# Light attention on one core: a step's three projections in one run, the output product in one run, and the next batch's rows turned behind the transposes

## The reference

```python
def local_attn(x, Wqkv, Wout):            # H = 8 heads of 64, windows of W = 64 rows
    q, k, v = jnp.split(x @ Wqkv.T, 3, axis=-1)
    q, k, v = map(towin, (q, k, v))
    ke, ve = (expand(k), expand(v))       # own window and its two neighbours
    sim = jnp.einsum('bhnid,bhnjd->bhnij', q, ke) * SCALE
    sim = jnp.where(valid, sim, -1e9)
    attn = jax.nn.softmax(sim, axis=-1)
    o = jnp.einsum('bhnij,bhnjd->bhnid', attn, ve)
    return o @ Wout.T
light = local_attn(_ln(x, ln_w, ln_b), Wqkv, Wout_l)
out = ... + light                          # and a "heavy" part on routed rows
```

## Time and profile before

| | |
|---|---|
| median of 3 runs | 1851.25 us (1850.41 to 1852.17) |
| span of the profiled execution | 1853.5 us; no other time of that execution is given |
| mean granted clock of TensorE | 0.970 |
| busy: PE, PEld, DVE, ACT, POOL | 90%, 69%, 78%, 78%, 41% of the span |
| light stage f1, first to last copy of `late` | 503.9 to 999.1 us |
| light stage f2, first to last copy of `late` | 1245.8 to 1732.2 us |

### The profile page before, as it was taken

How to read it: one execution, slowest core, us unless ns; L and a number is a source line. 1 busy time by engine, 2 the same in 40 slices (tenths; PEclk the granted TensorE clock), 3 DMA queues, 4 the chain that set the end, 5 groups by cost and what they waited for, 6 DMA issues and landing times. The chain is left out here.

```text
span 1853.5 us, 67967 instructions
## 1 busy us (share of the span) xinstructions
PE 1676.8 (90%) x27513; PEld 1287.6 (69%) x27513; DVE 1449.6 (78%) x3461; ACT 1437.3 (78%) x4100; POOL 753.0 (41%) x842
## 2 busy tenths in 40 slices
PE   3888898886899999999997996879999999999797
PEld 1444444443688888888886774658888888888686
DVE  8999999998677678877887766747777777789674
ACT  4989999996788888888774666658888888877464
POOL 2010000000255444455446866425454545455694
PEclk7999999998999999999999997989999999999999
DMA  6565556551001010101012000000101010001211
GB/s 194 140 155 146 149 124 148 132 149 28 13 15 25 14 26 14 26 14 26 14 26 48 2 2 1 1 12 15 25 14 26 15 25 18 22 14 25 48 47 47
DMA packets 80040, 91.95 MB, mean 50 GB/s; under 512 B 11696, under 2 KB 67984, under 8 KB 79728
## 3 DMA queue, kind: packets, MB, share of 16 engines
q1 hardware_dynamic: 78432, 87.15, 19.0%
q10 hardware_dynamic: 1296, 0.44, 0.1%
HBM read 39.68 MB, written 31.10 MB: 38 GB/s over the span
## 5 line engine op out<-in xcount | busy, mean ns | idle before, releaser
L1519 POOL TENSOR_TENSOR f1l_pn<-f1l_p,f1l_rs 128x512 f32<-128x512 f32 (+1 forms) x256 | 207.9, 834 | 259.3 <-DVE f1l_rs L1206 258.2
L1519 POOL TENSOR_TENSOR f2l_pn<-f2l_p,f2l_rs 128x512 f32<-128x512 f32 (+1 forms) x256 | 207.9, 834 | 248.8 <-DVE f2l_rs L1206 248.7
L1078 ACT ACTIVATE f2l_p<-f2l_sm,f2l_nb 128x192 f32<-128x192 f32 x512 | 214.7, 444 | 43.9 <-DVE f2l_nb L1199 43.9
L1078 ACT ACTIVATE f1l_p<-f1l_sm,f1l_nb 128x192 f32<-128x192 f32 x512 | 214.8, 444 | 42.0 <-DVE f1l_nb L1199 42.0
L417 PE MATMUL r_acc<-r_pr,r_vp 128*32 128x128 f32 (+2 forms) x3584 | 197.9, 338 | 6.9 <-DVE r_pr L630 6.0
L527 ACT ACTIVATE r_pr<-r_far 128x1536 f32<-128x1536 f32 x128 | 195.4, 1526 | 3.3 <-PE r_far L401 3.0
L622 DVE SCALAR_TENSOR_TENSOR r_pr<-r_pr,k_lo,r_cap 128x512 f32<-128x512 f32 x256 | 180.7, 746 | 11.0 <-ACT r_pr L527 10.9
L630 DVE TENSOR_SCALAR r_pr<-r_pr,k_hi,k_lo 128x768 f32<-128x768 f32 x256 | 164.5, 684 | 0.0
L527 ACT ACTIVATE r_pr<-r_near 128x1024 f32<-128x1024 f32 x128 | 139.6, 1091 | 1.1 <-PE r_near L388 1.1
L1524 POOL MEMSET k_rtz<- 128x132 f32 x1 | 0.2, 208 | 337.3 <-POOLq L688 337.3
L417 PEld LDWEIGHTS r_acc<-r_pr,r_vp 128*32 128x32 f32 x3584 | 89.1, 112 | 49.7 <-issue 31.2
(11 more groups left out here) (505 smaller groups left out, 5158.7 us busy)
## 6 DMA issues: line engine op xcount, KB each, us to landing
rbf_rows<-r_part SPq DMA_DIRECT2D x112, 128.0 KB, 2.3
r_qs<-rbf_rows SPq DMA_DIRECT2D x60, 192.0 KB
r_ks<-rbf_rows SPq DMA_DIRECT2D x60, 192.0 KB
f1l_vs<-f1l_vv SPq DMA_DIRECT2D x64, 128.0 KB, 2.4
f2l_vs<-f2l_vv SPq DMA_DIRECT2D x64, 128.0 KB, 2.4
rbf_rows<-r_part SPq DMA_DIRECT2D x16, 384.0 KB, 3.1
rbf_rows<-r_part SPq DMA_DIRECT2D x16, 256.0 KB, 3.2
out<-k_x SPq DMA_DIRECT2D x8, 512.0 KB, 3.2
```

What stands on the lines that cost most here:

```text
L1078: ins = nc.scalar.activation(p[:, u % 2, k, :], sm[:, u % 2, k // 2, k % 2 * PW:(k % 2 + 1) * PW], ACT.Exp, bias=nb[:, u % 2, k:k + 1], ac ...
L1519: ins = nc.gpsimd.tensor_tensor(pn[:, u % 2, at:at + HU * w].rearrange("p (k c) -> p k c", k=HU), p[:, u % 2, :, cols], r.broadcast_to([P, ...
```

## The change

On TensorE the three projections of a step now come first and one after another, into three banks: `pj`, `tp` and `xa[:, 1]`. The transposes of unit a then wait until `tp` has been emptied again by ScalarE, and the values of unit a wait for `xa[:, 1]`. The four chunks of the output product are one run into the first columns of `pj`. The transposes of unit b follow, and with i = 2 `turn_x`, now into `pj`. On ScalarE the first two copies out of the projections stand together ahead of the second exponential, the third one exponential later. On VectorE the residual stands behind the copies of unit a in every step.

```diff
         def bank(b, k):
             if b == 0 and (k <= 2 * HP or not C):
                 return (pj[:], tp[:], xa[:, 0, :], xa[:, 1, :])[k % 4]
-            return tp[:] if k == 0 else pj[:]
+            if b == 0 or k == 0:
+                return tp[:] if b == 1 else pj[:]
+            return (xa[:, 1, :], pj[:], tp[:])[k % 3]
+
+        def out_bank(t):
+            return pj[:, 0:P] if t < T - 1 else xa[:, 1, 0:P]
...
             def use(b, k):
                 at, par = bank(b, k), b % 2
+                t = NT * (b - 1) + (k - 1) // 3
                 if b == 0 and (k <= 2 * HP or not C):
                     wait(pe, s_pe, k - 4)
+                elif b == 0:
+                    pe.wait_ge(s_pe, k - 1)
+                elif k % 3 == 1:
+                    if t == 0:
+                        pe.wait_ge(s_pe, USES)
+                    wait(pe, s_la, t - 1)
+                    if t % NT == TURN_AT + 1 and b + 1 < B:
+                        pe.wait_ge(s_xe, b + 2)
+                elif k % 3 == 2:
+                    if t == 0:
+                        pe.wait_ge(s_xe, 2)
+                    wait(pe, s_pt, 2 * t)
                 else:
-                    pe.wait_ge(s_pe, USES * b + k - 1)
+                    if t == 0 and C:
+                        pe.wait_ge(s_re, 1)
+                    wait(pe, s_ov, 2 * t)
...
             def turn(n):
...
                 pe.wait_ge(s_nm, n + 1)
                 wait(pe, s_pt, n)
+                if u % 2 == 0 and b + 1 < B:
+                    pe.wait_ge(s_pe, USES * (b + 1) + 3 * (u // 2) + 2)
...
             def values(n):
...
-                if u % 2 == 0:
-                    wait(pe, s_la, NT * b + i)
+                if u % 2 == 0 and b + 1 < B:
+                    pe.wait_ge(s_pe, USES * (b + 1) + 3 * i + 3)
...
             def step(t):
                 b, i = t // NT, t % NT
                 more = b + 1 < B
-                ahead = i == TURN_AT and b + 2 < B
                 if more:
-                    use(b + 1, 3 * i + 1)
+                    for k in range(1, 4):
+                        use(b + 1, 3 * i + k)
                 turn(2 * t)
-                output(t - 1, (0,) if ahead else (0, 1))
-                if more:
-                    use(b + 1, 3 * i + 2)
-                if not ahead:
-                    output(t - 1, (2, 3))
+                output(t - 1)
                 turn(2 * t + 1)
-                if ahead:
-                    output(t - 1, (1,))
-                if more:
-                    use(b + 1, 3 * i + 3)
-                if ahead:
-                    output(t - 1, (2, 3))
+                if i == TURN_AT and b + 2 < B:
                     turn_x(b + 2)
                 values(2 * t)
...
             def step(t):
...
-                if soon:
-                    exps(2 * t + 2, (1, 2))
-                if more:
-                    leave(b + 1, 3 * i + 1)
-                if soon:
-                    exps(2 * t + 2, (3,))
-                    exps(2 * t + 3, (0, 1))
-                if more:
-                    leave(b + 1, 3 * i + 2)
-                if soon:
-                    exps(2 * t + 3, (2, 3))
+                if more:
+                    leave(b + 1, 3 * i + 1)
+                    leave(b + 1, 3 * i + 2)
+                if soon:
+                    exps(2 * t + 2, (1,))
                 if more:
                     leave(b + 1, 3 * i + 3)
+                if soon:
+                    exps(2 * t + 2, (2, 3))
+                    exps(2 * t + 3, (0, 1, 2))
                 if i == TURN_AT and b + 2 < B:
                     leave_x(b + 2)
+                if soon:
+                    exps(2 * t + 3, (3,))
                 leave_late(2 * t)
```

More of the change, by code:

```diff
@@ L731, in stage_light @@
         pj = ps("pj", [P, BANK])
-        XS, XO = 2 * P, 2 * P
+        XS = 2 * P
         SCALE = float(DH) ** -0.5
@@ L861, in turn_x @@
                 elif b > 1:
-                    pe.wait_ge(s_pt, UNITS * (b - 2) + 2 * TURN_AT + 2)
+                    pe.wait_ge(s_la, NT * (b - 2) + TURN_AT)
                 pe.wait_ge(s_z, b + 1)
@@ L920, in values @@
                     pe.wait_ge(s_vs[u // 2], 32 * (b + 1))
-                if C and n == 0:
-                    pe.wait_ge(s_re, 1)
-                if u % 2 == 0:
-                    wait(pe, s_la, NT * b + i)
+                if u % 2 == 0 and b + 1 < B:
+                    pe.wait_ge(s_pe, USES * (b + 1) + 3 * i + 3)
                 wait(pe, s_oe, n)
@@ L947, in values, with output @@
                 mm.then_inc(s_pv, 1)
-            def output(t, chunks):
+            def output(t):
                 if t < 0:
                     return
[L952 to L955, removed]
+                b, i = (t + 1) // NT, (t + 1) % NT
+                pe.wait_ge(s_oe, 2 * t + 2)
+                if b + 1 < B:
+                    pe.wait_ge(s_pe, USES * (b + 1) + 3 * i + 1)
+                else:
+                    wait(pe, s_la, t)
+                for c in range(HP):
+                    mm = nc.tensor.matmul(out_bank(t), ot[:, t % 2, c, :], K["wout_l"][:, c * P:(c + 1) * P],
                                           start=(c == 0), stop=(c == HP - 1))
-                if chunks[-1] == HP - 1:
-                    mm.then_inc(s_w, 1)
+                mm.then_inc(s_w, 1)
             turn_x(0)
@@ L1033, in places @@
                 pe.wait_ge(s_tk, LASTK + 1)
-                pe.wait_ge(s_pe, USES * B)
+                pe.wait_ge(s_la, T - 1)
                 for j in range(NT):
@@ L1041, in _ @@
             places()
-            output(T - 1, (0, 1, 2, 3))
+            output(T - 1)
         @block.scalar
@@ L1229, in residual @@
                 dve.wait_ge(s_w, t + 1)
-                nc.vector.tensor_tensor(K["x"][:, t, :], K["x"][:, t, :], xa[:, 1, XO:XO + P], ALU.add).then_inc(s_la, 1)
+                nc.vector.tensor_tensor(K["x"][:, t, :], K["x"][:, t, :], out_bank(t), ALU.add).then_inc(s_la, 1)
             def route_shift(k):
@@ L1458, in step @@
                 leave_turned(2 * t)
+                if t:
+                    residual(t - 1)
                 if soon:
                     reciprocals(2 * t + 2)
-                late = t % NT == TURN_AT and t // NT + 2 < B
-                if t and not late:
-                    residual(t - 1)
                 if finding:
@@ L1466, in step @@
                 leave_turned(2 * t + 1)
-                if late:
-                    residual(t - 1)
                 if soon:
```

## The result

The changed kernel takes 1947.06 us (median of four, 1943.48 to 1952.86) against 1850.98 us (1850.41 to 1852.17) for the kernel before: a ratio of 1.0518, 95% interval 1.0503 to 1.0533. It is slower by 96.1 us. The forecast was slower by 74 us, in a range of 1883 to 1955 us. The direction and the mechanism hold, and the size is 22 us short. The measurement still lies in the forecast's range, but what filled it up wasn't in the forecast.

The account below looks back on a forecast made before the run. TensorE's list, with a round trip through VectorE, was taken as the bound. Longer steps add 81.7 us in both stages, 8 us are given back: 1851.25 + 74 = 1925 us, range 1883 to 1955.

Parts of the forecast that it names:

- The bound: In the light stages, TensorE's instruction list, including the round trip through VectorE's copy of unit b's corner, sets the time.
- The length of a step: First projection to unit a's values: up 0.79 us (i 0, 1), 0.15 (i 2), 0.95 (i 3), 2.68 a batch.
- five places: After the first projection's start: unit a's transposes 2.39 us, corner 2.88; unit b's transposes 4.14, corner 4.61; unit a's values 5.60.
- the wait for ScalarE: Unit a's transposes wait for ScalarE's copy out of `tp`, starting at 2.39 us instead of 2.18.
- the hidden `turn_x`: For i = 2, `turn_x` moves into the 0.99 us gap before unit a's values and is hidden; step grows only 0.15 us.
- What is given back: VectorE's longer idle time absorbs 4 us of f1's extra work, search steps near both stages' ends another 4: 8 us off.
- The edits costed at nothing: Waits for `late`, the residual and the third copy, and moved `leave_x`, residual and DMA starts: no time added.
- rivals 1 and 2: The two rivals setting the range: two smaller waits cost nothing (1879 us, 0.11); more waits than seen (1961 us, 0.06).
- rival 3: TensorE's clock falls to half in one step of ten: 84 us more, 2009 us; chance 0.04.
- Rival 1: Waits for ScalarE's copy out of `tp` and VectorE's copy of unit a cost nothing: 1879 us; chance 0.11.
- Rival 4: ScalarE, not TensorE, sets the step, and the copy of unit b's corner is hidden: faster, 1808 us; chance 0.04.
- Rival 5: Nothing changes, because the run of projections gains what the gap before unit a's values costs; chance 0.03.

Follow-up runs that it names:

- e3_fill: The changed kernel with four unused transposes of a constant between unit b's corner and unit a's values, in three steps of four: 1957.68 us, ratio 1.0569.
- e8_third_back: The changed kernel with banks exchanged and the third projection back between unit b's transposes and unit a's values, except for i = 2: 1884.88 us, ratio 1.0182.
- e2_banks: The changed kernel with banks `tp` and `pj` exchanged, so unit a's transposes wait for the first projection's copy, not the second's: 1919.53 us, ratio 1.0359.
- e12_turnx: The changed kernel with `turn_x` behind unit a's values instead of ahead, and its copy on ScalarE behind `late`: 1966.09 us, ratio 1.0605.
- e7_spread: The changed kernel with banks exchanged, unit a's scores before its values, third projection behind unit a's transposes, next first projection before unit b's values: 1861.13 us, ratio 1.0055.
- e4_output: The kernel before with only the output product's four chunks in one run, ahead of the second projection, in their old bank: 1859.43 us, ratio 1.0038.
- e11_pair: The changed kernel with both units' scores ahead of both units' values: 2024.16 us, ratio 1.0918.
- e9_mixed: The kernel before with the second projection in `xa[:, 1]` right behind unit a's transposes and the output product in one run: 1865.83 us, ratio 1.0068.
- e10_shift: The changed kernel with 48 extra transposes of a constant at the start of f2 only: 1951.17 us, ratio 1.0526.

## Why the prediction was right in direction and 22 us short

- **The bound.** TensorE's list with VectorE's round trip in it was read rightly. e3_fill shows that the gap is idle and that VectorE ends it, and e8_third_back against e2_banks that one projection in it gives 35 us back.
- **The length of a step.** All five places were right within 0.04 us, and a batch's growth was 2.72 for 2.68 us. The fresh start, the run's 2.18 us, the wait for ScalarE (e2_banks) and the hidden `turn_x` (e12_turnx) each have a run or a row for it.
- **"What is given back".** This term was about right. Of f1's extra work 5.1 us were given back where I took 4, and of the search steps near the stages' ends 2.8 us in f2, some 5.6 in both, where I took 4 without a row. The row at 1620.51 is such a step.
- **What I left out.** These are the pauses: 14.6 us more than before by the count of idle stretches, some 26 by the length of the steps. The kernel before hardly shows them, 6 of 1.6 us in both stages. Without them the two stages would have grown by about 70 us, near the 74 of the forecast; with them the growth is 95.5. That the measurement lies within the range owes something to luck: the range was set by rivals 1 and 2, not by pauses.
- **The edits costed at nothing.** ScalarE's third copy starts at 1289.38 us and is over well before the values at 1292.41, and no row of waits names the residual ahead of the projections. No cost of theirs was found.
- **The clock.** It is 1.00 in both stages, so rival 3 is out. By the rule of the Trainium skill, TensorE: Matmul & The Clock Gate, section "A second HAM failure mode: psum-queue depth-cycling", this kernel should have lost more than the sum to a swinging clock. The trace doesn't agree: its granted clock is 1.00 in both windows above, and no fall of it lies between the first and last copy of `late` in f1 or f2.
- **The rivals.** Rival 1 fell with e2_banks. Rival 2 gave 1961, not far from the measurement, but for a reason that isn't there: the regular steps have no further wait. Rival 4 fell with the row at 1292.41: the copy isn't hidden. Even e7_spread, with both trips covered, is 0.55% over the kernel before. Rival 5 is out with the 5.2%.

What stays open is why some arrangements have pauses and others don't. e4_output (one of 0.2 us in f2), e7_spread (none) and e11_pair (one of 0.6) are nearly free of them like the kernel before, while e9_mixed, whose list differs little from before, has 17. That they belong to the fetching of instructions is argued from two facts, their end at 2.2 to 2.8 us behind a packet and the shift in e10_shift, in f2 and not in f1. It isn't shown by a run that takes the fetching away.

## What to carry to other kernels

Before you join pieces of work into one run, write down which round trip through another engine each piece covers where it stands. Here a fresh start costs some 0.1 us (the first two matmuls of a run start 0.33 us apart, the later ones 0.23), a round trip through VectorE 0.6 us of idle time, and there was a second trip behind the first. Look in the tail of the program, where the covering work has run out: rows of the last batch gave the places in the changed step within 0.04 us. And when a sum seems to close, hold it against the length of the single steps too: here two omitted terms, each of some 11 or 12 us, hid one another.

## What the runs showed of the hardware

**Pauses behind instruction packets.** TensorE stops for 0.1 to 1.4 us amid bursts of small matmuls and goes on 2.2 to 2.8 us after a 16 KB packet of the instruction queue starts, in the changed kernel mostly every five to six steps. By idle stretches they make 8 us a stage there, and up to 12 in e3_fill. The Trainium skill, Runtime: NRT & Kernel Launch, section "Instruction fetch mechanics", says that crossing such a block is mostly hidden. Most of the 74 packets of f2 are, as it says, but by the length of the steps the rest cost some 13 us a stage more than before, 26 us together or 1.3% of the changed kernel's time.

**A fall of the clock within a step.** In e11_pair the clock fell after TensorE had stood still for 0.62 and 0.94 us in one step (rows above). Two stretches of it, the second with the 0.96 us pause alone:

```profile
1450.00:1455.00 5.00, 5.00 (x46) 3.99 (x47) 2.70 (x6) 2.92 (x10) 0.00 (x0) 0.66 0.01 2
1469.00:1474.00 5.00, 3.96 (x54) 3.03 (x47) 3.23 (x7) 3.88 (x12) 1.11 (x2) 1.00 0.00 0
```

In the first one the mean is 0.66, and the projections stand 0.43 us apart instead of 0.23: that is half clock, 1.2 instead of 2.4 GHz. In the second they run at full clock. It is the only fall between f2's first and last copy of `late` in that kernel and lasts 3.4 us; f1 has two such falls, the first after 1.59 us of idle time, the second after 0.96 and 0.78. The 10.2 us at half clock cost some 5 us, an estimate, so the clock isn't why the forecast for e11_pair was short. The kernel before has one fall of 3.4 us as well, at 610.8 us in f1, after TensorE had waited 2.12 us. In the changed kernel 0.61 us of idle time a step never did this in f1 or f2.
